# Context kept in SBUF, other homes for the key parts, a two-slot score ring and turned maxima, in a twelve-stage perceiver kernel

## Time and profile before

| | |
|---|---|
| median of 3 runs (lowest to highest) | 843.14 us (842.65 to 843.39) |
| the profiled execution | 843.88 us |
| its span in the profile | 842.1 us |
| TensorE busy | 558.0 us, 66% |
| VectorE busy | 416.1 us, 49% |
| ScalarE busy | 326.1 us, 39% |
| GpSimd busy | 145.3 us, 17% |
| bytes moved | 44.48 MB, HBM read 29.25 MB |
| mean granted clock of TensorE | 0.70 of full speed |

### The profile page before, as it was taken

How to read it: one execution, slowest core, us unless ns; L and a number is a source line. 1 busy time by engine, 2 the same in 40 slices (tenths; PEclk the granted TensorE clock), 3 DMA queues, 4 the chain that set the end, 5 groups by cost and what they waited for, 6 DMA issues and landing times. The chain is left out here.

```text
span 842.1 us, 11473 instructions
## 1 busy us (share of the span) xinstructions
PE 558.0 (66%) x4652; PEld 369.1 (44%) x4652; DVE 416.1 (49%) x690; ACT 326.1 (39%) x377; POOL 145.3 (17%) x191
## 2 busy tenths in 40 slices
PE   4789997688773997234820450582579678499857
PEld 3566565574321564112300450571458322156556
DVE  4442002544797001454699999536543479800042
ACT  0224994212593996000540030000112149489710
POOL 3004000000000000105888991000300000000000
PEclk9576997757896899555865555565555579689956
DMA  7225904002610000403000000000700063050000
GB/s 193 67 62 121 389 2 116 0 1 56 145 35 0 2 4 8 108 0 116 0 0 0 1 0 0 0 1 0 215 1 1 18 144 73 1 226 2 3 0 2
DMA packets 14182, 44.48 MB, mean 53 GB/s; under 512 B 2913, under 2 KB 11617, under 8 KB 13030
## 3 DMA queue, kind: packets, MB, share of 16 engines
q1 hardware_dynamic: 14130, 43.75, 18.3%
HBM read 29.25 MB, written 0.03 MB: 35 GB/s over the span
## 5 line engine op out<-in xcount | busy, mean ns | idle before, releaser
L230 POOL TENSOR_TENSOR rstd<-rstd,minus_half 64x1 f32<-64x1 f32 x20 | 10.9, 544 | 592.3 <-DVE rstd L238 592.3
L2297 PE MATMUL psum<-l2x_pick,wide 128*128 128x64 f32 x196 | 42.3, 422 | 87.5 <-DVE l2x_pick L2410 87.5
L668 PE MATMUL psum<-keys_t,values 128*32 128x128 f32 x2352 | 97.5, 285 | 3.0 <-ACT keys_t L730 2.8
L2297 PEld LDWEIGHTS psum<-l2x_pick,wide 128*128 128x128 f32 x196 | 42.0, 333 | 88.1 <-DVE l2x_pick L2410 88.1
L668 PEld LDWEIGHTS psum<-keys_t,values 128*32 128x32 f32 x2352 | 57.1, 111 | 35.9 <-issue 28.6
L718 ACT ACTIVATE experts<-psum 128x896 f16<-128x896 f32 x84 | 69.6, 928 | 7.8 <-PE psum L635 7.5
L730 ACT ACTIVATE keys_t<-psum,l3x_exp_gain 128x1024 f32<-128x1024 f32 x49 | 54.4, 1114 | 14.3 <-PE psum L658 14.2
L730 ACT ACTIVATE keys_t<-psum,l0x_key_scale 128x1024 f32<-128x1024 f32 x49 | 54.4, 1115 | 9.4 <-PE psum L658 9.2
L730 ACT ACTIVATE keys_t<-psum,l1x_exp_gain 128x1024 f32<-128x1024 f32 x49 | 54.4, 1115 | 1.2 <-PE psum L658 0.9
L887 DVE TENSOR_TENSOR experts<-experts 128x1792 f16<-128x1792 f16 x38 | 40.6, 1087 | 3.6 <-ACT experts L718 1.8
L2398 DVE MAX8 l2x_best<-values 128x8 f32<-128x6272 f32 x6 | 40.2, 6692 | 0.1
(11 more groups left out here) (730 smaller groups left out, 1066.2 us busy)
## 6 DMA issues: line engine op xcount, KB each, us to landing
wide<-keys_t SPq DMA_DIRECT2D x108, 112.0 KB, 2.2
wide<-in_ctx_t SPq DMA_DIRECT2D x4, 1680.0 KB, 12.2
experts<-in_experts SPq DMA_DIRECT2D x1, 4608.0 KB, 14.4
experts<-in_experts SPq DMA_DIRECT2D x1, 4096.0 KB, 14.9
wide<-in_ctx_t SPq DMA_DIRECT2D x4, 672.0 KB, 5.2
keys_t<-in_ctx_tiles SPq DMA_DIRECT2D x1, 2352.0 KB, 9.7
experts<-in_experts SPq DMA_DIRECT2D x1, 2048.0 KB, 17.9
wide<-keys_t SPq DMA_DIRECT2D x36, 56.0 KB, 1.9
```

The costliest lines, as they stand in the source:

```text
L230: nc.gpsimd.tensor_tensor(out, base, exponent, ALU.pow).then_inc(*mem.pool_done.mark(event))
L668: last = nc.tensor.matmul(ps[32 * quarter:32 * quarter + 32, O_BANKS[pair // 4], 0:2 * T], mem.values[:, at:at + 32], probs[:, t % PROBS, ...
L2297: last = nc.tensor.matmul(ps[:, 1 + t // TPB, at * T:(at + 1) * T], S[:, r, t * 128:(t + 1) * 128], pick[:, r, :], start=False, stop=r == ...
```

## The change

- `ctx_t` gets a buffer of its own with 98 rows, the last one for the mask's bias. It is loaded once; the three later loads, their waits and the second fill of the ones are gone.
- The fp16 parts of the keys move from `keys_t` to `experts`; `keys_t` is gone. A smaller `ring` holds `probs`, `squares`, the copies for the maxima, the experts' hidden layers, the tiles of the context and the buffers of the small attentions. Packs of late stages share buffers with early ones and are loaded later: two in stage 4, three at the start of stage 7.
- `stage_cross_attention` is split into `stage_first_attention` and `stage_long_attention` (stages 4 and 10). In the latter the score ring has two slots, the sums of all pairs lie in bank 4 (cleared by one product), and the tail of the maxima is new. The experts of stage 12 are loaded before the maxima. The code could also take the maxima in chunks of the keys; with `MAX_SUPERS = [7]` there is one chunk, and that code does nothing.
- The mask's bias is made in stage 5 as [49, 128] and brought to row 97 by a transfer. In stage 7 the sine stands behind ScalarE's copies, `a` and `aT` are computed early, the sum of the chosen comes from 32 exponentials on ScalarE, the mask-multiply is in seven pieces that TensorE follows, ScalarE copies the turned blocks, and the convolution takes four triangular steps.

The core of the diff (lines that only move or rename are left out):

```diff
-        self.ctx_t = self.wide[0:CTX + 1, KEYS:2 * KEYS]
-        self.keys_t = sb("keys_t", [128, KEYS])
+        self.ctx_t = sb("ctx_t", [CTX + 2, KEYS])
+        self.ring = sb("ring", [128, KT_TILES * CTX])
...
+AFTER = {"l2x": "l0a", "l3x": "l0x", "l2a": "l1x", "l2f": "l1f", "l3a": "l1a"}
...
-    for pack in ["l1x", "l1a", "l1f", "l2x", "l2a", "l2f", "l3x", "l3a", "l3f"]:
+    for pack in ["l1x", "l1a", "l1f", "l3f"]:
         load_pack(mem, sp, pack)
...
-                sp.wait_ge(scores_ready, KT_TILES)
-                load_context(mem, sp)
```

Stages 4 and 10, new functions in full where the text speaks of them:

```diff
+    NUMERATOR_BANK, DEN_BANK, Y_BANK, O_BANK = 1, 2, 0, 4
+    SLOTS = (5, 6, 7)
+    RING, PROBS, COPIES = 2, 4, 3
...
+                for semaphore in stacked:
+                    sp.wait_ge(semaphore, 16 * PER_BATCH)
+                if level == 1:
+                    load_pack(mem, sp, "l2x")
+                    load_pack(mem, sp, "l3x")
+                if level == 3:
+                    sp.wait_ge(*dve_done.at("Q_stack"))
+                    sp.dma_start(mem.experts[:, :], mem.dram["experts3"]).then_inc(mem.loaded["experts3"], 16)
...
+                def turn_top(k):
+                    pe.wait_ge(top_ready, k + 1)
+                    for b in range(2):
+                        bank = slot((q_ready, 2 * k + b + 1))
+                        for j in range(4):
+                            last = nc.tensor.matmul(ps[:, bank, j * 128:(j + 1) * 128], turn[:, 4 * b + j, :],
+                                                    ident16[:, :], start=True, stop=True)
+                        last.then_inc(top_turned, 1)
...
+                def scores(t):
+                    u, j, pair, k = t // TPS, t % TPS, 2 * (t % RING), chunk_of[t]
+                    pe.wait_ge(*stacked_with(u))
+                    pe.wait_ge(q_ready, 2 * k + 2)
+                    if t >= RING:
+                        pe.wait_ge(probs_ready, t - RING + 1)
...
+                def weigh(t):
+                    k = chunk_of[t]
+                    if t == starts[k]:
...
+                        nc.tensor.matmul(ps[:, O_BANK, 0:4 * T], zeros16[:, 0:128], zeros16[:, :], start=True, stop=False)
+                    pe.wait_ge(probs_ready, t + 1)
+                    for pair in range(PAIRS):
+                        quarter, half, at = pair % 4, pair // 4, t * TILE_VALUES + pair * PAIR
+                        last = nc.tensor.matmul(
+                            ps[32 * quarter:32 * quarter + 32, O_BANK, 128 * half:128 * half + 128],
+                            mem.values[:, at:at + 32], probs[:, t % PROBS, 2 * T * pair:2 * T * (pair + 1)],
+                            start=False, stop=t == ends[k] - 1 and half == 1)
...
+                v.memset(turn[:, :, :], 0.0)
+                v.memset(zeros16[:, :], 0.0)
+                step(v.tensor_copy(ident16[:, :], ident))
...
+                def raise_top(k):
+                    step(v.tensor_scalar(lower[:, :], top[:, k, :], -1.0 / BIAS_ROW, None, ALU.mult))
+                    step(v.tensor_copy(turn[:, :, 96], lower[:, :]))
+                    v.tensor_tensor(turn[:, :, 97], lower[:, :], turn[:, :, 96], ALU.subtract).then_inc(top_ready, 1)
...
+                    for b in range(2):
+                        dve.wait_ge(top_turned, 2 * k + b + 1)
+                        bank = SLOTS[next(slots) % len(SLOTS)]
+                        v.tensor_copy(Q_stack[96:98, k, :, :].rearrange("p g n -> p (g n)")[:, 512 * b:512 * b + 512],
+                                      ps[96:98, bank, :]).then_inc(q_ready, 1)
...
+                n = HALF
+                while n > 56:
+                    n //= 2
+                    step(v.tensor_tensor(folded[:, :, :, 0:n], folded[:, :, :, 0:n], folded[:, :, :, n:2 * n], ALU.max))
+                for s in range(2):
+                    ins = v.tensor_reduce(rows_max[:, :].rearrange("p (g s) -> p g s", s=2)[:, :, s],
+                                          folded[:, s, :, 0:n], AX_X, ALU.max)
```

The first copied part of each half is written into `folded` at once, so 19 folds remain of 21. Stage 7 and stage 8:

```diff
@@ stage 7, SP
-                sp.dma_start(mask8, mem.dram["context_mask"]).then_inc(masks_loaded, 16)
+                for name in ["l2a", "l2f", "l3a"]:
+                    load_pack(mem, sp, name)
                 sp.dma_start(token8[:, :], mem.dram["token_mask"].to_broadcast([C, T])).then_inc(masks_loaded, 16)
@@ stage 7, ScalarE
-                state_kernel.act(act)
...
+                state_kernel.act(act)
                 for r in range(R):
                     act.wait_ge(*dve_done.at(f"max{r}"))
                     nc.scalar.activation(S[:, r, :], S[:, r, :], ACT.Exp, bias=minus_max[:, r:r + 1])\
                         .then_inc(*act_done.mark(f"exp{r}"))
+                    act.wait_ge(*dve_done.at(f"best{r}"))
+                    nc.scalar.activation(best_exp[:, :, :], best[:, :, :], ACT.Exp, bias=minus_max[:, r:r + 1],
+                                         accum_out=total[:, r:r + 1]).then_inc(*act_done.mark(f"total{r}"))
@@ stage 7, VectorE
-                v.tensor_scalar(mask_row, mask8, 1.0, 1e30, ALU.subtract, ALU.mult)\
...
-                    dve.wait_ge(*act_done.at(f"exp{r}"))
-                    v.scalar_tensor_tensor(out=S[:, r, :], in0=left, scalar=CHOSEN, in1=S[:, r, :],
-                                           op0=ALU.is_le, op1=ALU.mult, accum_out=total[:, r:r + 1])\
...
+                    dve.wait_ge(*act_done.at(f"total{r}"))
                     step(v.reciprocal(inverse[:, r:r + 1], total[:, r:r + 1]))
                     v.tensor_scalar(pick[:, r, :], mem.w("consts", "mean_heads"), inverse[:, r:r + 1],
                                     None, ALU.mult).then_inc(*dve_done.mark(f"picks{r}"))
+                    dve.wait_ge(*act_done.at(f"exp{r}"))
+                    for b in range(BLOCKS):
+                        keys = slice(b * TPB * 128, min(KEYS, (b + 1) * TPB * 128))
+                        v.scalar_tensor_tensor(out=S[:, r, keys], in0=left[:, keys], scalar=CHOSEN, in1=S[:, r, keys],
+                                               op0=ALU.is_le, op1=ALU.mult).then_inc(kept, 1)
...
+                for times, lags in [(slice(lo, lo + STEP), lo + STEP) for lo in range(0, T, STEP)]:
...
+                    step(v.tensor_tensor(products[:, times, 0:lags], window,
+                                         spread(mem.kernel_reversed[:, T - lags:T], 1, [C, STEP, lags]), ALU.mult))
+                    step(v.tensor_reduce(mixed[:, times], products[:, times, 0:lags], AX_X, ALU.add))
@@ stage 7, TensorE, second product of the heads
+                        if at == 0:
+                            pe.wait_ge(kept, r * BLOCKS + t // TPB + 1)
@@ stage 8, SP and GpSimd
-                load_context(mem, sp)
...
-                pool_ones_row(mem)
-                pool.wait_ge(mem.ones_row, 2)
                 pool_value_ones(mem, mem.value_ones)
```

More of the change, by code:

```diff
@@ L24 @@
 from contextlib import ExitStack
-from itertools import islice
+from itertools import count, islice
 import concourse.bass as bass
@@ L1370, in __init__, with ring @@
         self.QT, self.KT, self.V = sb("QT", [C, T]), sb("KT", [C, T]), sb("V", [T, C])
-        self.Qbd = sb("Qbd", [C, HG, T])
-        self.S = sb("S", [128, 2 * G, T])
-        self.P = sb("P", [128, 2 * G, T])
+        at = iter(range(self.RING, mem.ring.shape[1], HG * T))
+        def ring(n):
+            first = [next(at) for _ in range(n)][0]
+            return mem.ring[:, first:first + n * HG * T].rearrange("p (n t) -> p n t", t=T)
+        self.Qbd, self.weighted, self.S, self.P = ring(1), ring(1), ring(2), ring(2)
         self.top, self.total = sb("top", [128, 2 * G]), sb("total", [128, 2 * G])
-        self.PT = sb("PT", [T, H * T])
-        self.weighted = sb("weighted", [C, HG, T])
+        self.PT = ring(4).rearrange("p n t -> p (n t)")[0:T, :]
         self.OT = sb("OT", [C, T])
```

892 lines of the change are left out of this document (586 added, 306 removed).

## The result

The changed kernel takes 834.0 us (833.76 to 834.4), the kernel before 843.26 us in the same comparison: a ratio of 0.9876 (0.9835 to 0.9917), 9.3 us faster. Forecast were 817.9 us and 807 to 827; the direction was right, the size was not.

The account below looks back on a forecast made before the run. Twelve stages run serially on one core, read by each engine's order of time, the top-32 stage taking 203.9 of 842.1 us. Terms summed to -25.3: 843.88 to 818.6, less 0.7 to the median, 817.9 us; range 807 to 827.

Parts of the forecast that it names:

- the rival in which two slots cost something: Attention over all keys: the loop's period grows by 0.05 to 0.2 us over 98 tiles, 823 to 838 us; chance 0.08.
- Scores of the top-32 stage: Stage 7's start: the first match-replace starts near 407.6 instead of 415.62, -8.0 us (ends -10.3 and -2.5).
- Masking of the first rows: Stage 7: seven multiplies take turns with GpSimd's products, 14.9 us instead of 10.96, +3.9 us (ends -3.4 and +4).
- The rival in which VectorE keeps the port: Stage 7's first masking: VectorE runs its seven multiplies without yielding to GpSimd, 7.3 us less, 810.6 us; chance 0.30.
- Masking of the second rows: Stage 7: one small multiply instead of a whole one stands before TensorE's last products, -5.7 us (ends -5.9 and -5.0).
- After the pooling: Stage 7: `aT` leaves the chain, -0.4 us, and the triangular products have fewer elements, -2.0 us.
- Local attention: Stage 8: GpSimd's fill of the row of ones goes from beside VectorE's normalisation, -4.6 us (ends -5.0 and -4.1).
- Maxima turned: Stages 4 and 10, last fold to first weighted scores: 6.9 us instead of 11.3, -4.4 each, -8.8 in all.
- Score ring, loop: Stages 4 and 10: two score slots keep the loop's pace and only its head changes, +0.3 us (ends -1 and +2).
- The rival of the hidden transfers: Whole kernel: the change only frees transfers that were hidden, another wait ends as late, 843 us; chance 0.03.
- that of the low clock under the scores: Stage 7's scores: the clock stays low, the first half takes 18.8 us instead of 13.9, 822.8 us; chance 0.12.

Follow-up runs that it names:

- e2: The kernel before with only its first fold slot taken from two folds to three: 861.1 us against 844.25, ratio 1.0188.
- e1: The changed kernel with no fold after the first reduction instead of one: median 825.7 us, ratio 0.9759.
- g3: The changed kernel with later folds, undivided first-rows multiply and token mask first, where a fold waits only for the last fold into its half: 806.6 us, ratio 0.9560.
- e4: The changed kernel with three score slots instead of two in stages 4 and 10 and the sums in bank 7: 835.1 us, ratio 0.9869.
- f5: The changed kernel with the token mask's transfer issued ahead of the three packs at the start of stage 7: 831.1 us, ratio 0.9853.
- f7: The changed kernel with the state kernel's sine back ahead of ScalarE's copies of the scores: 846.05 us, ratio 1.0043.
- e3: The changed kernel with the first rows masked by one multiply of 6,272 instead of seven of 896: 829.1 us, ratio 0.9811.
- g2: The changed kernel with GpSimd's fill of a 6,272-element row back at the start of stage 8: 839.1 us, ratio 0.9936.
- g1: The changed kernel with later folds, undivided first-rows multiply, token mask first, and 34 plus 5 filler products on TensorE in stages 4 and 10: 807.0 us, ratio 0.9575.
- f8: The changed kernel with later folds, undivided first-rows multiply, token mask first, and 24 filler products on TensorE in stages 4 and 10: ratio 0.9600.

## Why the prediction was right and wrong

**Wrong: a term that is not in the sum.** The prediction went through stages 4 and 10 from the last fold on ("from the last fold (ends 260.73) to the first weighted scores"). The phase ahead of it, 38.4 and 39.6 us, was taken as unchanged without a word, although the change makes 19 folds of 21 and moves the slots. It grew by 8.0 and 7.5 us. e2 puts this on one number of the fold order, and e1 takes back 13.7 of the 15.5. Of the other 1.8, the wait between folds of different halves (0.23 us a period) is the part of stage 4: without it, in g3, the phase took 38.6 us, as good as before. In stage 10 the runs don't separate it from the clock. The first slot, now empty, costs nothing: from the first scores to the third reduction pass 10.6 us in e1 (227.24 to 237.83) and 10.7 before (222.30 to 232.96). No rival foresaw this mechanism, and the range did not hold it. 834.0 lies inside the band of the rival in which two slots cost something (823 to 838), but by another cause, as e4 shows. 834.0 less 15.5 is 818.5, and the forecast was 817.9. That this is so near is partly luck, since the other terms were off by up to 2 us each way, as follows.

**Scores of the top-32 stage**, forecast -8.0: measured -6.2, within the ends. The mask landed 6.3 us into the stage, where 4.5 was taken (389.5 is 4.8 into it; bound 7.3). The term counted one transfer's 4.6 us from the start of the stage. The three packs' issues came first, so the mask's own transfer was issued 1.7 us into the stage, at 388.81, and took its 4.6 us from there. f5 wins 3.2 by moving it. TensorE ran its first three chunks at the low clock and the others at the full one (four were taken). f7 shows that the sine gave 1.5 of it directly. The error of 1.8 here and that of 1.7 in the next term, the other way, cancel: that stage 7 as a whole came out at -12.5 for -12.2 is luck.

**Masking of the first rows**, forecast +3.9: measured +2.2 (13.1 against 10.96). The handovers came one for one, with five long products and two short ones as counted, but a multiply and a product took 2.08 us together instead of the 2.33 taken (0.99 and 1.34). (The parts of the sum give 7.7 and 15.0, not 7.6 and 14.9.) The rival in which VectorE keeps the port is out: 12.57 us, not 6.9. The Trainium skill (SBUF — State Buffer, "SBUF: two separate sides") describes the shared pair as an exclusive lock for a whole instruction; the trace agrees (one product of GpSimd took 7.82 us beside a multiply of 6.68 in e3). Who gets it when both have work is what the runs add: the one that waited, every time in these rows. So an instruction in pieces loses a turn at each cut.

**Masking of the second rows**, -5.7: 7.2 became 1.6, -5.6. **After the pooling**, -2.4: the eight convolution steps took 6.8 us (559.52 to 566.34) instead of 8.9, -2.1, and `aT` is gone from the chain. (Eight starts of 0.2 are 1.6, not the 1.4 of the sum.) **Local attention**, -4.6: -4.5, with 0.94 us left of the normalisation as bounded; g2 confirms the cause.

**Maxima turned**, -4.4 each: 11.3 to 6.4, -4.9 each. The folds took 2.18 (2.10 counted), the two reductions 0.68 (0.8), the eight products 1.03 (bounds 0.9 and 2.6).

**Score ring, loop**, +0.3: the pace stayed at 1.12 us and e4 finds 0.3 to 0.5 us a stage at the head, but stage 10's loop took 2.2 us more (727.55 to 790.8 against 738.99 to 800.0) and stage 4's 0.2, 2.4 in all, above the upper end of 2. TensorE after and then before, from the turned maxima of stage 10 on (stretch, length, busy, clock, DMA share, GB/s):

```profile
725.40:732.00 6.60, 5.04 (x37) 0.50 0.00 0
732.00:737.00 5.00, 5.00 (x56) 0.55 0.02 3
```

```profile
735.80:739.00 3.20, 1.88 (x5) 0.50 0.00 0
739.00:743.00 4.00, 4.00 (x30) 0.50 0.86 295
743.00:747.00 4.00, 4.00 (x64) 0.87 1.02 442
```

By the shares of these stretches TensorE was back at the full clock at 736.5, 11.1 us after it resumed, and before at 744.0, 8.3 after. More of that stretch lies in the loop now, too: from the turned products to the loop pass 2.1 us instead of 3.2. In stage 4 the two kernels are nearly alike in this (the loops took 62.8 and 63.0 us). Why the clock came back sooner in stage 10 of the kernel before stays open. g1 shows that it can be held. The rival of the hidden transfers (843 us) is out; that of the low clock under the scores too.

## What to carry to other kernels

Where an order is written out by hand, removing two items is not only removing their time: work out which item now stands in each slot and what the slot's neighbour waits for. A phase whose engines all show slack (here TensorE 35, VectorE 34 and ScalarE 37 of 46 us) may be bound by that order, and the brackets behind its rows say where. Cutting an instruction so that a consumer can start early costs a turn per cut if another engine wants the same access; cut only where the consumer is on the path.

## What the runs showed that was not expected

- One number in a fold order is worth 16.9 us of 844 by the medians, 15.3 by the two stages (e2).
- The same code of stage 1 took 138.8 to 146.6 us, with TensorE's granted clock at 0.65 or 0.50 from 40 to 60 us.
- TensorE came back to the full clock between 7.4 (stage 10 of e2) and 11.5 us (stage 4 of g3) after it resumed behind the tail of the maxima; with 34 and 5 filler products it never left it there (g1), with 24 and a stand of 2.4 us it did (f8).
- The place of one sine on ScalarE, 0.31 us, changed VectorE's masking by 7.4 us (f7), by which GpSimd products stood beside it.
